# Attention inside an AdaLN block: the scores of each head's second block run in the stage of the first, with a fifth place for transposed probabilities and rearranged lists

## The reference

```python
q = jnp.einsum('bpm,hmd->bphd', x, Q_w) + Q_b      # likewise k and v
logits = jnp.einsum('bqhd,bkhd->bhqk', q, k) / math.sqrt(d_head)
logits = jnp.where(causal_mask, NEG, logits)
scores = jax.nn.softmax(logits, axis=-1)
attn = jnp.einsum('bhqk,bkhd->bqhd', scores, v)
out = jnp.einsum('bqhd,hdm->bqm', attn, O_w) + O_b
```

## Time and profile before

| | us |
|---|---|
| median of 3 runs | 2029.73 |
| lowest, highest | 2028.84, 2031.98 |
| the profiled execution | 2029.64 |
| its span | 2027.6 |
| PE busy | 1935.7 (95%) |
| DVE busy | 1418.3 (70%) |
| ACT busy | 1122.8 (55%) |
| POOL busy | 572.5 (28%) |
| DMA queue of SyncE | 64.0% of 16 engines' span |

### The profile page before, as it was taken

One profiled execution on the slowest core, in us unless ns is written; L12 is line 12 of the kernel. 1 busy time (PEld: TensorE's weight loads), 2 busy tenths in 40 slices (PEclk: granted clock), 3 DMA queues, 4 the chain that ended last, 5 costly groups with the idle time before them and its releaser, 6 DMA issues.

```text
span 2027.6 us, 33851 instructions
## 1 busy us (share of the span) xinstructions
PE 1935.7 (95%) x9823; PEld 1143.6 (56%) x9825; DVE 1418.3 (70%) x3588; ACT 1122.8 (55%) x1643; POOL 572.5 (28%) x583
## 2 busy tenths in 40 slices
PE   5899999999999999999999999689999999999997
PEld 2444444444444444444444444368877778787786
DVE  5687797797797797797797797646545833333476
ACT  3676776776776676676676686413333144354311
POOL 4531230330330330330330311632000132232265
PEclk8899999999999999999999999799999999999999
DMA  7377777777777777777777777874431098999666
GB/s 241 79 164 176 172 174 176 172 173 176 174 171 176 175 171 176 176 170 176 175 170 176 172 157 161 210 206 143 125 110 32 1 299 283 322 299 306 221 203 186
DMA packets 932181, 366.15 MB, mean 181 GB/s; under 512 B 754800, under 2 KB 885920, under 8 KB 932128
## 3 DMA queue, kind: packets, MB, share of 16 engines
q1 hardware_dynamic: 921888, 331.93, 64.0%
q0 software_dynamic: 10240, 33.56, 5.4%
HBM read 138.86 MB, written 41.94 MB: 89 GB/s over the span
## 4 chain that ended last, share of the span: by engine, by line
PE 72%; DVE 8%; issue 6%; DMA 4%; ACT 3%; POOL 3%; SPq 3%; DVEq 0%; ACTq 0%; POOLq 0%
PE gen L1734 10%; PE gen L1735 10%; PE gen L1736 10%; PE strip L1734 6%; PE strip L1736 6%; PE strip L1735 6%; PE pv L1734 5%; PE pv L1735 5%; PE pv L1736 5%; PE strip L2053 5%; DMA wd_sb<-in_L_ffn_Wd 2%; PE strip L2060 2%; DVE p_lo L1310 2%; SPq L501 2%; DVE exps L1286 1%
## 5 line engine op out<-in xcount | busy, mean ns | idle before, releaser
L955 ACT ACTIVATE exps<-exps,nbias,cols_now 128x128 f32<-128x128 f32 (+15 forms) x256 | 329.8, 1289 | 167.5 <-DVE cmin L1296 165.5
L1310 DVE SCALAR_TENSOR_TENSOR p_lo<-exps,rinv,p_hi 128x512 f16<-128x512 f32 (+3 forms) x256 | 404.9, 1608 | 23.8 <-ACT p_hi L964 23.3
L964 ACT ACTIVATE p_hi<-exps,rinv 128x512 f16<-128x512 f32 (+3 forms) x256 | 333.9, 1352 | 35.1 <-issue 13.7
L1286 DVE TENSOR_SCALAR_CACHE_REDUCE exps<-strip 128x512 f32<-128x512 f32 x384 | 250.9, 687 | 126.5 <-PE strip L1736 123.9
L1734 PE MATMUL strip<-kT_hi,qT_hi 128*128 128x512 f16 (+3 forms) x640 | 221.4, 351 | 28.2 <-DVE kT_lo L1239 16.6
L1734 PE MATMUL pv<-pT,v 128*128 128x512 f16 (+3 forms) x640 | 223.3, 349 | 4.5 <-DMA pT<-p_lo 4.5
L1735 PE MATMUL strip<-kT_lo,qT_hi 128*128 128x512 f16 (+3 forms) x640 | 224.3, 350 | 0.0
L1735 PE MATMUL pv<-pT,v 128*128 128x512 f16 (+3 forms) x640 | 223.3, 349 | 0.0
L1736 PE MATMUL strip<-kT_hi,qT_lo 128*128 128x512 f16 (+3 forms) x640 | 221.7, 350 | 0.0
L1736 PE MATMUL pv<-pT,v 128*128 128x512 f16 (+3 forms) x640 | 219.8, 349 | 0.0
L758 POOL TENSOR_TENSOR wq_f<-wq_f,fac 128x512 f32<-128x512 f32 x15 | 15.6, 1041 | 707.5 <-PE gen L1736 707.5
(11 more groups left out here) (285 smaller groups left out, 4302.1 us busy)
## 6 DMA issues: line engine op xcount, KB each, us to landing
at_dram<-at_f SPq DMA_DIRECT2D x64, 256.0 KB, 2.6
wg_sb<-in_L_ffn_Wg SPq DMA_DIRECT2D x64, 256.0 KB
wu_sb<-in_L_ffn_Wu SPq DMA_DIRECT2D x64, 256.0 KB
wd_sb<-in_L_ffn_Wd SPq DMA_DIRECT2D x64, 256.0 KB
yb_dram<-yb SPq DMA_DIRECT2D x64, 256.0 KB
a_f<-at_dram SPq DMA_DIRECT2D x58, 256.0 KB, 2.8
pT<-p_hi SPq DMA_TRANSPOSE x320, 2.7
pT<-p_lo SPq DMA_TRANSPOSE x320, 2.8
```

The source lines that it names most:

```text
L955: nc.scalar.activation(row, row, ACT.Exp, bias=nbias[:, t:t + 1], scale=cols_now[:, LOGIT_UP:LOGIT_UP + 1], accum_out=rsum[:, t:t + 1]).th ...
L964: nc.scalar.activation(p_hi16[:, 0:j + 1, t, :], row, ACT.Copy, scale=rinv[:, t:t + 1]).then_inc(p_hi, 1)
L1286: nc.vector.tensor_scalar(exps[:, t, 512 * ch:512 * ch + w], strip[u % STRIPS][:, 0:w], 1.0, None, ALU.mult, ALU.max, accum_out=cmax[:, t, ...
L1310: nc.vector.scalar_tensor_tensor(p_lo16[:, 0:j + 1, t, :], row, rinv[:, t:t + 1], p_hi16[:, 0:j + 1, t, :], ALU.mult, ALU.subtract).then_i ...
```

## The change

The scores of block 1 move from stage 1 to the end of stage 0. With that:

- `PTS` becomes 5, with a fifth place `pT4` in memory that is free during attention. The last head uses four places as before (`PTS_LAST`), since the fifth overlaps with buffers of the output projection.
- TensorE, stage 0: scores of block 0, projections q, k, v of block 1, scores of block 1, value sums of block 3 of the head before, bounds. Stage 1: projections q and k of block 2, value sums of block 0, projection v of block 2.
- ScalarE and VectorE get a function `second_block` with all of block 1's rows, called in stage 0. In stage 0 the four `p_hi` (and `p_lo`) of block 0 come ahead of the halves of block 1's keys. Stage 1 holds only the halves of block 2's projections and `attended` of block 0, which on ScalarE stands between those of the keys and those of the values.
- SyncE, stage 0: transposes of block 0, values of block 0, transposes of block 1 with the values of block 1, and then `store_at` of block 3 of the head before.

The core of the diff:

```diff
-        STRIPS, GENS, PTS = 4, 3, 4
+        STRIPS, GENS, PTS, PTS_LAST = 4, 3, 5, 4
...
@@ SyncE
             def stage(h, j, prev, nxt):
+                if j != 1:
+                    turn_first_rows(h, j)
+                    turn_last_rows(h, j)
                 if j == 0:
                     turn_values(h, 0, h)
-                turn_first_rows(h, j)
-                turn_last_rows(h, j)
+                    turn_first_rows(h, 1)
+                    turn_last_rows(h, 1)
                 if prev is not None:
                     store_at(*prev)
                 if nxt is not None and nxt[1] > 1:
...
-            turn_first_rows(H - 1, 1)
-            turn_last_rows(H - 1, 1)
             for hd in range(6):
                 load_wo(hd)
@@ ScalarE
-                act.wait_ge(at_scaled, h * 2 + 2)
+                act.wait_ge(at_scaled, h * 2 + 4)
...
+            def second_block(h):
+                exp_row(h, 1, 0)
+                exp_row(h, 1, 1)
+                probs_hi(h, 1, (h, 0), 0)
+                probs_hi(h, 1, (h, 0), 1)
+                exp_row(h, 1, 2)
+                exp_row(h, 1, 3)
+                gen_hi_of("v", 1, h)
+                probs_hi(h, 1, (h, 0), 2)
+                probs_hi(h, 1, (h, 0), 3)
...
                 if j == 0:
-                    exp_row(h, j, 2)
-                    exp_row(h, j, 3)
-                    gen_hi_of("q", nxt[1], nxt[0])
-                    gen_hi_of("k", nxt[1], nxt[0])
+                    for t in range(TB):
+                        exp_row(h, j, t)
+                    gen_hi_of("q", 1, h)
                     for t in range(TB):
                         probs_hi(h, j, prev, t)
+                    gen_hi_of("k", 1, h)
+                    second_block(h)
+                    attended(*prev)
+                    take_at_scale(h)
+                elif j == 1:
+                    gen_hi_of("q", 2, h)
+                    gen_hi_of("k", 2, h)
+                    attended(*prev)
+                    gen_hi_of("v", 2, h)
@@ VectorE
             def stage(h, j, nxt, ahead=True):
...
+                    gen_out_of("q", 1, h)
+                    for t in range(TB):
+                        probs_lo(h, j, t)
+                    gen_out_of("k", 1, h)
+                    second_block(h)
+                    if ahead:
+                        take_bounds(h + 1, bounds)
+                        factors(h + 1)
+                elif j == 1:
+                    gen_out_of("q", 2, h)
+                    gen_out_of("k", 2, h)
+                    gen_out_of("v", 2, h)
@@ TensorE
             def stage(h, j, prev, nxt, bounds=True, ahead=True):
-                score(h, j, bounds)
                 if j == 0:
-                    project("q", *reversed(nxt))
-                    project("k", *reversed(nxt))
-                    if ahead and prev is not None:
+                    score(h, 0, bounds)
+                    for kind in "qkv":
+                        project(kind, 1, h)
+                    score(h, 1, bounds)
+                    sum_values(*prev)
+                    if ahead:
                         next_bounds(h)
-                if prev is not None:
+                elif j == 1:
+                    project("q", 2, h)
+                    project("k", 2, h)
                     sum_values(*prev)
...
+                    project("v", 2, h)
```

More of the change, by code:

```diff
@@ L166, in adaln_block @@
         pT_at = a.at
-        pT = a.place("pT", [P, PTS, 2, TB, TB, P], F16)
+        pT = [a.place(f"pT{i}", [P, 2, TB, TB, P], F16) for i in range(PTS_LAST)]
+        pT.append(SbufMap(nc, pad_at).place(f"pT{PTS_LAST}", [P, 2, TB, TB, P], F16))
         spare_at = a.at
@@ L363, in adaln_block @@
         GROUPS = QB * (QB + 1) // 2
-        SLOT_USES = [len(range(i, GROUPS, PTS)) for i in range(PTS)]
         def nth(kind, j, h):
@@ L380, in groups_before, with is_last, slot_of @@
             return j * (j + 1) // 2
-        def slot_of(j, g):
-            return (groups_before(j) + g) % PTS
+        def is_last(h):
+            return isinstance(h, int) and h == H - 1
+        def slot_of(j, g, h):
+            return (groups_before(j) + g) % (PTS_LAST if is_last(h) else PTS)
         def slot_turned(j, g, h):
             n = groups_before(j) + g
-            return h * (4 * 16 * SLOT_USES[n % PTS]) + 4 * 16 * (n // PTS + 1)
+            return h * (4 * 16 * (GROUPS // PTS)) + 4 * 16 * (n // (PTS_LAST if is_last(h) else PTS) + 1)
         def slot_free(n, h):
-            before = n + GROUPS - PTS if n >= PTS else n + (GROUPS - 1 - n) // PTS * PTS
+            slots = PTS_LAST if is_last(h) else PTS
+            before = n + GROUPS - slots if n >= slots else n + PTS
             return h * GROUPS + (before + 1)
@@ L399, in adaln_block @@
         NSTRIP = strips_before(QB)
-        assert NG % GENS == 0 and NSTRIP % STRIPS == 0
+        assert NG % GENS == 0 and NSTRIP % STRIPS == 0 and GROUPS == 2 * PTS
         def score_units(j):
@@ L499, in turn_pair @@
                 rows = (p_hi16, p_lo16)[part][:, g, 2 * r:2 * r + 2, :].rearrange("p t c -> p (t c)")
-                out = pT[:, slot_of(j, g), part, 2 * r:2 * r + 2].rearrange("p t k q -> p (t k) q")
-                sp.dma_start_transpose(out, rows).then_inc(p_turned[slot_of(j, g)], 16)
+                out = pT[slot_of(j, g, h)][:, part, 2 * r:2 * r + 2].rearrange("p t k q -> p (t k) q")
+                sp.dma_start_transpose(out, rows).then_inc(p_turned[slot_of(j, g, h)], 16)
             def turn_first_rows(h, j):
@@ L1329, in stage @@
[L1329 to L1331 removed]
+                    gen_out_of("q", 1, h)
[10 more added lines that the diff above has]
+                    gen_out_of("v", 2, h)
+                else:
+                    score_row(h, j, 0)
+                    score_row(h, j, 1)
+                    row_inverse(h, j, 0)
+                    if j == QB - 1:
+                        gen_out_of("v", QB - 1, h)
+                    score_row(h, j, 2)
+                    row_inverse(h, j, 1)
+                    score_row(h, j, 3)
@@ L1337, in stage @@
                         take_columns(h + 1)
-                probs_lo(h, j, 2)
-                probs_lo(h, j, 3)
-                if nxt is not None:
+                    probs_lo(h, j, 2)
+                    probs_lo(h, j, 3)
                     hn, jn = nxt
-                    if j > 0:
-                        gen_out_of("q", jn, hn)
-                        gen_out_of("k", jn, hn)
-                    if j == 0 and ahead:
-                        take_bounds(h + 1, bounds)
-                        factors(h + 1)
-                    if jn in (0, 2):
+                    gen_out_of("q", jn, hn)
+                    gen_out_of("k", jn, hn)
+                    if jn == 0:
                         gen_out_of("v", jn, hn)
@@ L1780, in score @@
                     u = strips_before(j) + n
-                    if j == 1 and n == STRIPS - 1 and bounds:
+                    if j == 2 and n == STRIPS - 1 and bounds:
                         pe.wait_ge(bound_out, h + 2)
@@ L1798, in sum_values @@
                         out = pv[:, P * t0:512].rearrange("p (t q) -> p t q", q=P)
-                        last = matmul3(out, v16[:, g, 0, kt, :], v16[:, g, 1, kt, :], pT[:, slot, 0, t0:TB, kt, :],
-                                       pT[:, slot, 1, t0:TB, kt, :], g == 0 and kt == 0, g == j and kt == TB - 1)
+                        last = matmul3(out, v16[:, g, 0, kt, :], v16[:, g, 1, kt, :], pT[slot][:, 0, t0:TB, kt, :],
+                                       pT[slot][:, 1, t0:TB, kt, :], g == 0 and kt == 0, g == j and kt == TB - 1)
                     last.then_inc(pv_group, 1)
```

66 lines of the change are left out of this document (35 added, 31 removed).

## The result

The changed kernel takes 2081.02 us (median of 4 runs, 2079.55 to 2084.19), the kernel before 2029.48 us in the same comparison (4 runs, 2028.84 to 2031.98): a ratio of 1.0253, with a 95% interval of 1.0239 to 1.0268. The profiled execution took 2084.19 us, its span is 2082.6.

A forecast was written before the change was run, and what follows sets the result against it. TensorE, busy 95% of the span, was taken as the bound, with SyncE's in-order queue as the deciding term. 2029.6 + 52 (14 heads) - 4 (last head) + 7 (clock) = 2085 us, range 2055 to 2120.

The forecast's parts named there:

- The late store: Block 2's fifth strip: TensorE waits 2.7 us per head because block 3's store leaves late in SyncE's queue, holding `at_f`.
- The keys of block 1: Block 1's scores: TensorE waits 1.54 us per head for the low keys, a wait that was not there before.
- The keys of block 2: Block 2's scores: the old wait of 0.83 us per head for `kT_lo` goes.
- The pace behind the wait: Strips after block 2's fifth: VectorE sets the pace, another 0 to 0.6 us per head, taken as 0.3.
- The clock: TensorE after the new wait: slower matmuls cost 0 to 2 us per head, taken as 0.5, +7 us in all.
- The case in which the clock falls in every head: Rival: same waits, plus 2.0 us lost per head at the lower clock, 2105 us, up to 2120; chance 0.12.
- The last head: Last head: SyncE gets through earlier to the output-weight loads, -4 us, bounds 0 and -6.
- 14 equal heads: Attention loop: 14 heads each 3.7 us longer, a period of 80.6 us, +52 us in all.
- the store comes in time: Rival: block 3's store lands early enough, the 2.7 and 0.3 us vanish, +6 us, 2036 us; chance 0.05.
- faster: Rival: the store lands in time and the `kT_lo` wait is also hidden, -16 us, 2014 us; chance 0.05.

The follow-up runs named there:

- Two experiments, one at each end of the link: Changed kernel with ScalarE's `attended` of block 0 behind block 2's `vT`, 2044.6 us; or SyncE's block 3 store ahead of block 1's last four transposes, 2044.39 us.
- the repaired kernels: Changed kernel with block 3's store and block 1's keys moved up, 2033.32 us; with the last head's output-weight loads also moved behind block 2's transposes, 2029.15 us.
- the fill: Changed kernel with eight unused 512-column projection matmuls added on TensorE between block 2's fourth and fifth strip, 2080.38 us.

## Why the prediction was right, step by step

- **The late store** (the 2.7 of the sum). Right in place and cause, and near in size. Shifted to the head of 390.62 the prediction's chain has the store at 424.1 and the first strip free at 429.4; they came at 423.47 and 428.8. Its first link was 0.5 us too long: `p_hi` of block 1 was released by the landing at 407.88, worked out as 408.4. The waits are 2.05 to 2.62 in the twelve middle heads, 2.31 on average, 0.4 under the forecast. Two experiments, one at each end of the link, take it away.
- **The keys of block 1** (+1.54): 1.40 in every middle head; with the keys moved 0.60 is left, as a wait for VectorE at block 1's fifth strip. But its price is conditional, which the sum did not say: alone it is worth nothing, since the store's wait takes it back; behind a cured store it is worth about 10 us.
- **The keys of block 2** (-0.83): no hole there any more.
- **The pace behind the wait** (0.3): holes of 0.06 and 0.28. They stay (0.15, 0.05 and 0.28) in the repaired kernels and belong to the order, not to the store.
- **The clock** (+7 of 0 to 28): a size that was off. It fell in six of twelve middle heads, as the prediction allowed ("not every such wait need do it"), and in both end periods; by the starts about 14 us, of which the fill could recover 7. The rows rule out that the waits' length alone decides: 2.14 brought half clock (head 227.79) and 2.58 did not (head 955.66). The case in which the clock falls in every head, 2105, did not come. The Trainium skill ("TensorE: Matmul & The Clock Gate", Part 1, "What's actually happening") says of the throttled state that it is the default and that activity releases it. The prediction took from this that each wait would be charged in full; in this trace six of the twelve middle heads were charged.
- **The last head** (-4): measured -6.4, in part by luck. SyncE does reach the loads earlier (32.9 us into the head, 37.9 before), and the waits of 5.86 for `kT_lo` and of 4.46 at block 2's value sums are gone. But the late store stalls this head too, which the sum left out: `at_f` waits 7.2 us for it and TensorE 4.25 at block 2's fifth strip. And reaching the loads earlier is not enough: with `attended` or the store moved the first load stands 34.1 and 35.1 us into the head, and the piece behind head 15's start takes 807.9 and 806.3 us, where the kernel before has 807.6 and the changed one 801.2. What differs in the rows is the time from the first load to block 2's transposes: 20.95 us before (1257.96 to 1278.91), 21.8 with `attended` moved, 21.2 with the store moved, and 17.0, 15.7 and 17.1 in the three kernels that keep the stall (the changed one, that with the keys moved, that with the fill). It follows GpSimd's splits (last section). That the stall helped the changed kernel there fits these rows; no run isolates it. Nor is all of these differences attention's: up to the last matmul of the output projection the piece takes 287.3 us before, 277.9 in the changed kernel, 284.0 with `attended` and 284.3 with the store moved. The rest, which no edit touches, takes 520 to 524 us in these four profiles.
- **14 equal heads**: the twelve middle ones have 80.84 against 80.6 + 0.5. The first and the last period are 3 us longer, which the sum did not have. It is the same chain behind a slower landing. In the first (head 143.99) block 0's last two transposes, issued at 157.71 and 159.06, land 5.0 and 4.5 us later, where the same two in head 390.62 take 2.7; so `p_hi` of block 1 starts 19.6 us into the head in place of 17.3, and the store goes out at 35.2 in place of 32.9. In the last (head 1197.86) the store itself takes 3.9 to land, in place of 2.7. Why these DMAs took longer stays open.

Errors of both signs met: 61.3 for 59, -6.4 for -4. Within the 61.3 too: the waits make some 47 where the sum had 52, and the clock 14 where it had 7. That the forecast came within 4 us is in part luck. The rivals "the store comes in time" and "faster" fell with the row at 426.24. The kernel with the store moved up is the first of them with its condition met, and the rival had priced it too low: 2036, 6 us over the kernel before, where 2044.4 and 13.5 over were measured. Two terms of its sum did not hold: it took away the pace term with the store, and that stays (0.49 in each head, 7 us); and of the 4 us of the last head, 1.3 came.

## What to carry to other kernels

Where an order is moved, follow what each in-order queue now does later, find the one buffer whose reuse hangs on it, and read what stands behind the instruction that waits for it: the damage is done to the neighbours in the list. A wait's price is what is left when the next wait on its path is gone, so repairs are tried together as well as alone. And a hole that moves a few strips when its cause is moved may belong to the pace of an engine and not to the order of its list.

## What the runs showed of the hardware

GpSimd and VectorE block each other in one combination, which the prediction did not look for. In the last head of the kernel with `attended` moved, GpSimd, then VectorE at the same time:

```profile
1281.59 0.61 POOL L852 CAST wo<-wq_raw 128x512 fp32r<-128x512 f32 x1
1282.28 1.27 POOL L854 TENSOR_TENSOR wo<-wq_raw,wo 128x512 fp32r<-128x512 f32 x1
1283.51 2.13 POOL L852 CAST wo<-wk_raw 128x512 fp32r<-128x512 f32 x1
1285.72 2.66 POOL L854 TENSOR_TENSOR wo<-wk_raw,wo 128x512 fp32r<-128x512 f32 x1
```
```profile
1282.32 2.85 DVE L1330 SCALAR_TENSOR_TENSOR p_lo<-exps,rinv,p_hi 128x1536 f16<-128x1536 f32 x1
```

The same `p_lo` with GpSimd idle, in the loop of the kernel with block 1's first row ahead:

```profile
571.97 1.81 DVE L1334 SCALAR_TENSOR_TENSOR p_lo<-exps,rinv,p_hi 128x1536 f16<-128x1536 f32 x1
```

The `p_lo` issued at 1282.32 takes 2.85 us: GpSimd's subtraction, begun 0.04 earlier, ends at 1283.55, and from there 1.62 are left of it. The cast issued at 1283.51 ends at 1285.64, 0.47 after `p_lo`, and takes 2.13 in place of 0.61. Each waits for the other's end. In the kernel before, the 60 `p_lo` of this size with GpSimd idle take 1.80 to 1.82 us, and the four beside GpSimd's splits 1.90 to 2.89. Beside VectorE's strip reads nothing of the kind is seen: the changed kernel's six casts from 1319.30 to 1328.82 take 0.60 or 0.61 while VectorE reads block 2's strips. The Trainium skill ("SBUF — State Buffer", "SBUF: two separate sides") calls the ports that the two engines share an exclusive lock, which VectorE takes for an operation with two inputs in SBUF; these rows agree (`exps` and `p_hi` are two such inputs, a strip is none). So a list on GpSimd has two speeds, by what VectorE does at that moment, and a chain through both changes when either is shifted.
